# Opening of a conditioned transformer block: first norm's modulation first, weights of queries and keys split first, two constant rows set by ScalarE

## The chip, the cores and the metric

The kernel runs on one core of one Trainium2 chip. The metric is the device time of one execution in microseconds. The kernel is timed several times, and the median counts.

The engines, as the profile names them: PE is TensorE, DVE is VectorE, ACT is ScalarE, POOL is GpSimd, SP is SyncE, which only issues DMAs here. Each runs its own list of instructions in order, and they wait for each other by semaphores.

## The reference

One transformer block whose norms are modulated by a condition vector. There are 8 batches of 512 rows of 256 features, 16 heads of 16, and a hidden layer of 1024, all in float32:

```
c6 = silu(c) @ Wc + bc                              # c 8x256, Wc 256x1536
sh_msa, sc_msa, g_msa, sh_mlp, sc_mlp, g_mlp = split(c6, 6)
xm = layernorm(x) * (1 + sc_msa) + sh_msa
q, k, v = xm @ Wq + bq, xm @ Wk + bk, xm @ Wv + bv
w = softmax(q/16 @ k^T) per head;  y = w @ v
x = x + g_msa * (y @ Wo + bo)
xm2 = layernorm(x) * (1 + sc_mlp) + sh_mlp
x = x + g_mlp * (gelu(xm2 @ W1 + b1) @ W2 + b2)
```

The first two of the six vectors of `c6` (shift and scale of the first norm) are needed for the first batch's queries and keys. The other four are needed later.

## The kernel before, in words

**Steps.** `schedule` runs `step(i, par)` on every engine for i from -2 to 8. In step i the engines work on three batches at once: attention of batch i (transposed scores, exponentials, products with V), row maxima of the scores of batch i+1, norm and projections of batch i+2; the hidden layer of batch i-1 is in it too. The steps -2 and -1 are the fill: step -2 projects batch 0, step -1 projects batch 1 and then computes the scores and row maxima of half of batch 0's heads and a few more.

**Precision.** Operands of the projections are split in two: a rounded part (`hi`, type fp32r) and the rest (`lo`), and three products are summed. The split of the weights `wqkvo` is a cast and a subtraction on VectorE (lines 878 and 880). Queries and keys are each written as three bfloat16 parts: ScalarE takes the first from PSUM (L518), VectorE forms the remainder (L970) and the second part (L973), GpSimd the third (L438). SyncE stores them to DRAM (`parts_scratch`, `write_parts`, three DMAs for each of four tiles, L315) and loads them again in another order as the stacks `qst` and `kst` (`load_stack`, L322), 96 partitions deep. Two further rows of the stacks hold the row maxima, in `qst`, and the constant -1, in `kst`; only the transposed scores read them.

**Opening.** Before the steps, in the order of each engine:

- SyncE loads c, the two halves of Wc (rows 0 to 127 into `vaug[0]`, rows 128 to 255 into `qst[0]`, which are free until batch 0's V and queries), x of batch 0 (`xa`), bc, Wq, Wk, Wv, Wo, four small biases, W1, W2, and bo and b2 broadcast. Then it waits for `c6` and stores it (L274), for the gates that are read back later. In step -2 it loads x of batch 1 into the same `xa` when the transposes of batch 0 are done (L280), then come the stores of the parts.
- GpSimd sets the identity and small constants, then the two rows of -1 in `kst[0]` (L375), then the ones in `vaug[1]` (L377). When the modulation is done it sets the ones in `vaug[0]` (L407). It also raises variances to the power -1/2 (`norm`, L393).
- TensorE transposes c (L559), multiplies with Wc (L565: three chunks of 512 columns, two matmuls each, banks 1 to 3), transposes `c6` (L570, twelve small ones) and the biases (L574).
- VectorE finishes the silu (L814, L816, L818; ScalarE's exponential L458 lies ahead), does batch 0's statistics (L828) and variance (L834 to L839), adds bc (L868, 8x1536), normalises (L847), copies the modulation vectors (L872), adds 1 to both scales (L875), splits all four weights, and copies the biases (L883).
- ScalarE waits for the last of these (`prep_dve` 7) and writes z of batch 0, the modulated norm, from the transposed rows in PSUM (`modulate`, L478).

In step -2 VectorE goes on with the casts and the subtraction of z (`z_hi` L904, `z_lo` L908), then with statistics and variance of batch 1, then with the remainders of batch 0 (`rest_of`), then it normalises batch 1. TensorE does the projections of queries and keys (L700, L705) and V (L552). ScalarE writes V and then the rounded parts of W1 and W2 (L527, L528). The order is written out by hand; no planner sets it.

## Time and profile before

| | us |
|---|---|
| runs: median of 3 | 781.13 |
| runs: lowest, highest | 777.75, 783.33 |
| profiled execution, its own time | 775.7 |
| its span in the trace | 773.8 |
| TensorE busy | 707.6 (91%) |
| VectorE busy | 582.3 (75%) |
| ScalarE busy | 384.3 (50%) |
| GpSimd busy | 222.3 (29%) |

The profile is one execution, and times within it are microseconds from the start of its span. TensorE's busy time is an upper bound of its work, since matmuls are pipelined and their ends are modelled. The granted clock of TensorE has two levels, 1.2 and 2.4 GHz, shown as 0.50 and 1.00. A busy share is a mean over stages, so the opening has to be read from the chain of waits and the timeline.

### The profile page before, as it was taken

Reading aid. Unit: us, or ns where it says so; the run is one execution under the profiler, and the core shown is the slowest. Engines: PE = TensorE matmul, PEld = TensorE weight load, DVE = VectorE, ACT = ScalarE, POOL = GpSimd, SP = SyncE. Lnnn points to the kernel's source line nnn. Section 1 sums busy time; section 2 is a strip of 40 time slices with the busy share of each in tenths; the row PEclk is TensorE's granted clock in tenths of the full one; section 3 lists DMA queues with packets and bytes.
Section 4 is the critical chain, followed back from the end, with each engine's and each line's share of the span. In section 5 each row is a group of like instructions: output and inputs, shape, how many; then the busy total and the mean of one; then the engine's idle time right before and its main releaser. Section 6 shows DMA issues by size and latency. Waiting matters only on the chain.

```text
span 773.8 us, 11775 instructions
## 1 busy us (share of the span) xinstructions
PE 707.6 (91%) x3967; PEld 382.9 (49%) x3967; DVE 582.3 (75%) x1015; ACT 384.3 (50%) x462; POOL 222.3 (29%) x163
## 2 busy tenths in 40 slices
PE   4678989769999999999999899999999998998986
PEld 1551222432268425772378225862478225812976
DVE  5769688859886898789887798789886976721463
ACT  0430556217752676347642775257633773298221
POOL 5245001200334031511253032512162022230444
PEclk9785799959999999999999999999999999999998
DMA  8489100681039302860067303840076102021110
GB/s 290 138 253 289 62 21 22 223 203 55 28 136 261 99 28 73 257 165 34 31 218 176 112 15 121 247 141 28 30 243 166 59 27 72 3 82 45 56 35 27
DMA packets 59558, 88.45 MB, mean 114 GB/s; under 512 B 6214, under 2 KB 47708, under 8 KB 56428
## 3 DMA queue, kind: packets, MB, share of 16 engines
q1 hardware_dynamic: 59500, 87.69, 37.0%
q8 instruction: 35, 0.57, 0.3%
q14 instruction: 23, 0.19, 0.1%
HBM read 49.35 MB, written 38.06 MB: 113 GB/s over the span
## 4 chain that ended last, share of the span: by engine, by line
issue 34%; PE 32%; DVE 14%; POOL 11%; DMA 5%; ACT 3%; SPq 1%; POOLq 0%; DVEq 0%; ACTq 0%
DVE mx L899 7%; PE ps L620 7%; PE ps L598 7%; PE ps L628 6%; PE ps L552 5%; POOL hl L445 4%; PE ps L759 3%; POOL prob L438 2%; PE ps L763 2%; DMA qst<-mrow 2%; ACT prob L500 1%; DMA kst<-parts_scratch 1%; POOL x L418 1%; POOL xd L431 1%; POOL zl L397 1%
## 5 line engine op out<-in xcount | busy, mean ns | idle before, releaser
L899 DVE TENSOR_REDUCE mx<-ps 128x1 f32<-128x512 f32 x512 | 335.4, 685 | 62.6 <-PE ps L598 56.4
L500 ACT ACTIVATE prob<-ps 128x1024 f32<-128x1024 f32 x256 | 247.9, 1022 | 156.5 <-PE ps L628 156.2
L598 PE MATMUL ps<-kst,qst 96*128 96x512 bf16 x512 | 196.2, 405 | 24.9 <-DVE mx L899 19.0
L628 PE MATMUL ps<-qst,kst 98*128 98x512 bf16 x512 | 150.4, 385 | 4.0 <-DMA qst<-mrow 2.4
L598 PEld LDWEIGHTS ps<-kst,qst 96*128 96x128 bf16 x512 | 45.5, 98 | 191.5 <-DVE mx L899 165.8
L620 PE MATMUL ps<-prob,vaug 128*32 128x512 f32 x1024 | 137.6, 609 | 0.5 <-ACT prob L500 0.3
L445 POOL TENSOR_TENSOR hl<-z,hh 128x512 fp32r<-128x512 f32 x64 | 82.3, 1287 | 137.3 <-DVE hh L1028 137.3
L539 ACT ACTIVATE z<-ps,bias_t 128x512 f32<-128x512 f32 x64 | 44.1, 689 | 134.5 <-PE ps L763 127.1
L393 POOL TENSOR_TENSOR rstd<-vare,mhalf 128x4 f32<-128x4 f32 x16 | 16.4, 1022 | 249.6 <-DVE vare L839 249.6
L628 PEld LDWEIGHTS ps<-qst,kst 98*128 98x128 bf16 x512 | 46.9, 99 | 70.1 <-ACT prob L500 26.6
L438 POOL TENSOR_TENSOR prob<-prob 128x512 bf16<-128x512 f32 x32 | 37.4, 1167 | 139.7 <-DVE prob L973 139.7
L552 PE MATMUL ps<-w_hi,hh 128*128 128x256 f32 x256 | 73.6, 288 | 0.3 <-POOL hl L445 0.3
L552 PE MATMUL ps<-w_hi,hl 128*128 128x256 f32 x256 | 72.0, 281 | 0.0
L552 PE MATMUL ps<-w_lo,hh 128*128 128x256 f32 x256 | 71.9, 281 | 0.0
L1028 DVE CAST hh<-z 128x512 fp32r<-128x512 f32 x64 | 37.0, 580 | 35.8 <-ACT z L539 35.8
L759 PE MATMUL ps<-zh,w_hi 128*128 128x512 f32 x128 | 60.5, 472 | 2.0 <-DVE zh L904 2.0
L759 PE MATMUL ps<-zh,w_lo 128*128 128x512 f32 x128 | 51.5, 402 | 0.0
L552 PEld LDWEIGHTS ps<-w_hi,hh 128*128 128x128 f32 x256 | 48.2, 188 | 2.9 <-POOL hl L445 0.7
L552 PEld LDWEIGHTS ps<-w_lo,hh 128*128 128x128 f32 x256 | 48.2, 188 | 1.8
L552 PEld LDWEIGHTS ps<-w_hi,hl 128*128 128x128 f32 x256 | 48.2, 188 | 0.0
L620 PEld LDWEIGHTS ps<-prob,vaug 128*32 128x32 f32 x1024 | 20.4, 108 | 46.1 <-issue 41.9
L478 ACT ACTIVATE z<-ps,mod 128x512 f32<-128x512 f32 x30 | 21.7, 774 | 39.9 <-DVE bias_t L883 18.5
(106 smaller groups left out, 854.4 us busy)
## 6 DMA issues: line engine op xcount, KB each, us to landing
parts_scratch<-prob SPq DMA_DIRECT2D x32, 384.0 KB, 2.9
qst<-parts_scratch SPq DMA_DIRECT2D x16, 768.0 KB, 9.1
kst<-parts_scratch SPq DMA_DIRECT2D x16, 768.0 KB, 14.0
parts_scratch<-prob SPq DMA_DIRECT2D x32, 256.0 KB, 3.1
y_scratch<-rb SPq DMA_DIRECT2D x32, 256.0 KB, 2.0
xa<-in_x_dram SPq DMA_DIRECT2D x8, 512.0 KB, 4.4
parts_scratch<-prob SPq DMA_DIRECT2D x32, 128.0 KB, 2.9
xd<-in_x_dram SPq DMA_DIRECT2D x8, 512.0 KB, 3.5
```

The source lines that it names most:

```text
L438: pool.tensor_tensor(parts[:, j, PART_AT[j // 2][2], :], rest[:, j % 2, :], parts[:, j, 1, :], ALU.subtract).then_inc(part_l, 1)
L445: pool.tensor_tensor(hl[:, j % HR, :], hb[:, j % HB, :], hh[:, j % HR, :].bitcast(F32), ALU.subtract).then_inc(hl_done, 1)
L478: act.activation(z_of(n, b)[:, k, :], ps[:, banks + k, :], ACT.Identity, bias=mod[:, 2 * shift + k, bass.ds(b, 1)], scale=mod[:, 2 * scale ...
L500: act.activation(prob[:, s % 2, 2 * p:2 * p + 2, :], ps[:, 2 * p:2 * p + 2, :], ACT.Exp, scale=1.0 / DH).then_inc(exp_done, 1)
L539: act.activation(hb[:, j % HB, :], ps[:, 4 + j % 2, :], ACT.Gelu, bias=b1_t[:, j:j + 1]).then_inc(gelu_done, 1)
L552: m = pe.matmul(out_, a, b, start=start and n == 0, stop=stop and n == 2, skip_group_check=True)
L598: pe.matmul(ps[:, banks[n % len(banks)], :], qst[1 - par][0:MROW, h, t * P:(t + 1) * P], kst[1 - par][0:MROW, h, :], start=True, stop=True ...
L620: m = pe.matmul(ps[32 * q:32 * q + 32, 4 + g % 2, :], vaug[par][:, kt, G * g + q, :], prob[:, s % 2, q, :], start=kt == 0, stop=kt == TT - ...
L628: m = pe.matmul(ps[:, q, :], kst[par][0:KROWS, G * g + q, kt * P:(kt + 1) * P], qst[par][0:KROWS, G * g + q, :], start=True, stop=True)
L759: pe.matmul(ps[:, 4 + j % 2, :], w1[n][:, k, f], zh_of(1, b)[:, k, :], start=k == 0 and n == 0, stop=False)
L899: dve.tensor_reduce(mx[:, t, h:h + 1], ps[:, banks[n % len(banks)], :], AXX, ALU.max).then_inc(max_done, 1)
L1028: dve.tensor_copy(hh[:, j % HR, :], hb[:, j % HB, :]).then_inc(hh_done, 1)
```

## The change

- `kst[0]`'s two rows of -1 are no longer filled by GpSimd. ScalarE copies them from a constant column of -0.5 with scale 2, behind its exponential; a semaphore `krows_set` says so, and TensorE waits for it before the first transposed scores.
- The load of x goes ahead of Wc. Wc is loaded in two parts of columns: 0 to 511 (the first norm's shift and scale) early, 512 to 1535 behind Wq, Wk and the biases. Wv and Wo follow it.
- The modulation is computed in two turns. Chunk 0 comes first, with its sum (8x512), its four transposes and its vectors. Chunks 1 and 2 are multiplied in step -2 between the projections of keys and V (banks 6 and 7), their sum (8x1024) stands on VectorE behind the last remainder of batch 0, ahead of batch 1's normalising, and their eight transposes behind V.
- The split of the weights is in two halves: queries and keys before step -2's z, values and output behind batch 1's variance, ahead of batch 0's remainders.
- ScalarE's z waits for the first norm's vectors only, no longer for the splits and biases.
- SyncE's store of `c6` moves into step -2, behind the stores of batch 0's parts and ahead of the first stack loads; these also wait for the second turn of the modulation, since `qst[0]` holds Wc till then.
- GpSimd's fill of ones in `vaug[0]` moves behind its work on batch 0's parts.
- The silu's product is written into `yc` and not into z. General counters are replaced by semaphores for each purpose.

```diff
+MOD_BANKS = (1, 6, 7)
...
@@ SyncE
             sp.dma_start(stage[0:NB, 1, 0:H], c).then_inc(c_loaded, 16)
+            sp.dma_start(xa[:], x[0].rearrange("(t p) f -> p t f", p=P)).then_inc(xa_loaded, 16)
             for k in range(KC):
-                sp.dma_start(wc_half[k], Wc[k * P:(k + 1) * P, :]).then_inc(wc_loaded, 16)
-            sp.dma_start(xa[:], x[0].rearrange("(t p) f -> p t f", p=P)).then_inc(xa_loaded, 16)
+                sp.dma_start(wc_half[k][:, 0:2 * H], Wc[k * P:(k + 1) * P, 0:2 * H]).then_inc(wc_loaded[0], 16)
...
+            qkvo_weights(0, Wq, wqkvo_loaded[0])
+            qkvo_weights(1, Wk, wqkvo_loaded[0])
...
+            for k in range(KC):
+                sp.dma_start(wc_half[k][:, 2 * H:], Wc[k * P:(k + 1) * P, 2 * H:]).then_inc(wc_loaded[1], 16)
+            qkvo_weights(2, Wv, wqkvo_loaded[1])
+            qkvo_weights(3, Wo, wqkvo_loaded[1])
...
-            sp.wait_ge(prep_dve, 4)
-            sp.dma_start(c6_scr[:], stage[0:NB, 1, 256:256 + 6 * H]).then_inc(c6_written, 16)
+            def modulation_rows():
+                sp.wait_ge(c6_added, 2)
+                sp.dma_start(c6_scr[:], stage[0:NB, 1, 256:256 + 6 * H]).then_inc(c6_written, 16)
...
+                    if early(i) and not later(i, 2, 1):
+                        modulation_rows()
+                        sp.wait_ge(c6_done, 2)
                     load_stack(i + 2, 0, 0)
...
@@ GpSimd
-            pool.memset(kst[0][MROW:KROWS, :, :], -1.0).then_inc(const_set, 1)
+            pool.memset(vaug[1][:, :, :, DH:], 1.0).then_inc(const_set, 1)
...
                     norm(0, 0)
-                    pool.wait_ge(prep_pe, 2)
-                    pool.memset(vaug[0][:, :, :, DH:], 1.0).then_inc(const_set, 1)
                     norm(0, 1)
...
                         mlp_weights()
+                    elif early(i):
+                        pool.wait_ge(c6_done, 2)
+                        pool.memset(vaug[0][:, :, :, DH:], 1.0).then_inc(const_set, 1)
...
@@ ScalarE
+            act.wait_ge(const_set, 1)
+            act.activation(kst[0][MROW:KROWS, :, :], mhalf[MROW:KROWS, 0:1].unsqueeze(2).broadcast_to([KROWS - MROW, NH, S]), ACT.Copy,
+                           scale=2.0).then_inc(krows_set, 1)
...
                     if not later(i, 2, 1):
-                        act.wait_ge(prep_dve, 7)
+                        act.wait_ge(mod_set, 2)
                     modulate(0, i + 2, 2, SH1, SC1)
...
@@ TensorE
+            def modulation(chunks):
+
+                pe.wait_ge(wc_loaded[min(chunks[0], 1)], 16 * KC)
+                for n in chunks:
+                    for k in range(KC):
+                        m = pe.matmul(ps[0:NB, MOD_BANKS[n], :], yc[:, 1, k * NB:(k + 1) * NB],
+                                      wc_half[k][:, n * 512:(n + 1) * 512], start=k == 0, stop=k == KC - 1)
+                m.then_inc(c6_done, 1)
...
+            pe.wait_ge(silu_done, 3)
+            modulation((0,))
+            turn_modulation(1, 0, 4)
...
                     if not later(i, 2, 1):
                         pe.wait_ge(w_split, 2)
-                        pe.wait_ge(prep_dve, 7)
...
+                    if not later(i, 2, 1):
+                        modulation((1, 2))
+                        pe.wait_ge(w_split, 4)
                     for t in range(TT):
...
+                    if not later(i, 2, 1):
+                        turn_modulation(2, 4, 12)
...
@@ VectorE
+            def split_weights(turn):
+
+                w = slice(2 * turn, 2 * turn + 2)
+                src = stage[:, 0, 1024 * turn:1024 * turn + 1024]
+                dve.wait_ge(wqkvo_loaded[turn], 32)
+                dve.tensor_copy(wqkvo[0][:, w].rearrange("p n c f -> p (n c f)"), src).then_inc(w_split, 1)
...
             variance(0, 0)
...
+            add_c6(1, 0, (1,))
             for t in range(TT):
                 normalise(0, 0, xa, t)
...
+            set_modulation(1, 0, 4, SC1)
+            split_weights(0)
+            dve.wait_ge(bias_turned, 1)
...
                     for t in range(TT):
                         statistics(0, 1, xa, t)
                     variance(0, 1)
+                    split_weights(1)
...
                 if has_a and not later(i, 2, 1):
+                    add_c6(2, 512, (6, 7))
                     for t in range(TT):
                         normalise(0, 1, xa, t)
+                    set_modulation(2, 4, 12, SC2)
```

## Rows read from the trace of the kernel before

**Rows 1.** The page, its head: span and instructions.
```profile
span 773.8 us, 11775 instructions
```

**Rows 2.** Chain of waits, 0 to 110 us: start, us, what it is.
```profile
41.98 10.72 DMA kst<-parts_scratch
...
53.18 20.42 DVE mx L899 x34
```

**Rows 3.** Timeline, opening: start, us, engine, line, operation, count [idle before it <- releaser].
```profile
1.62 6.92 POOL L375 MEMSET kst<- 2x8192 bf16 x1
...
2.10 0.43 SPq L256 DMA_DIRECT2D xa<-in_x_dram  x1
...
4.41 4.16 DVE L814 TENSOR_SCALAR z<-z 128x16 f32<-128x16 f32 x1 [4.41 <-ACT z L458]
...
9.12 1.88 PE L565 MATMUL ps<-vaug,z 128*8 128x512 f32 x2 [6.31 <-DVE z L818]
...
11.67 0.43 SPq L271 DMA_DIRECT2D b_b<-in_L_cond_b_dram  x1
...
12.16 1.02 PE L565 MATMUL ps<-vaug,z 128*8 128x512 f32 x2
...
15.79 1.75 DVE L868 TENSOR_TENSOR qst<-ps,qst 8x1536 f32<-8x1536 f32 x1 [4.21 <-PE ps L565]
...
17.47 1.36 DVE L847 TENSOR_SCALAR xa<-xa,mv,rstd 128x256 f32<-128x256 f32 x4
...
18.89 1.97 PE L580 MATMUL ps<-ident,xa 128*128 128x128 f32 x8 [0.32 <-DVE xa L847]
...
19.19 1.22 DVE L878 CAST wqkvo_hi<-qst 128x2048 fp32r<-128x2048 f32 x1
20.45 2.29 DVE L880 TENSOR_TENSOR wqkvo_lo<-qst,wqkvo_hi 128x2048 fp32r<-128x2048 f32 x1
...
22.86 1.45 ACT L478 ACTIVATE z<-ps,mod 128x512 f32<-128x512 f32 x2 [18.48 <-DVE bias_t L883]
```

**Rows 4.** Timeline, 24 to 56 us: batch 0's projections to the first score.
```profile
25.94 1.40 DVE L828 BATCH_NORM_STATS2 stats<-xa 128x6 f32<-128x256 f32 x4
...
28.03 1.01 POOL L393 TENSOR_TENSOR rstd<-vare,mhalf 128x4 f32<-128x4 f32 x1 [11.26 <-DVE vare L839]
28.95 1.26 ACT L518 ACTIVATE prob<-ps,bias_t 128x512 bf16<-128x512 f32 x2 [4.65 <-PE ps L705]
...
29.67 0.75 DVE L970 SCALAR_TENSOR_TENSOR prob<-ps,bias_t,prob 128x512 f32<-128x512 f32 x1 [1.72 <-ACT prob L518]
...
32.16 7.20 SPq L315 DMA_DIRECT2D parts_scratch<-prob  x12
...
35.40 2.21 DVE L847 TENSOR_SCALAR xa<-xa,mv,rstd 128x256 f32<-128x256 f32 x4
...
35.62 1.90 ACT L527 ACTIVATE w_hi<-kst 128x2048 fp32r<-128x2048 f32 x1
...
52.75 1.56 PE L598 MATMUL ps<-kst,qst 96*128 96x512 bf16 x5 [1.10 <-DMA kst<-parts_scratch]
```

**Rows 5.** Timeline of ScalarE, 79 to 95 us: exponentials of batch 0.
```profile
83.50 1.94 ACT L500 ACTIVATE prob<-ps 128x1024 f32<-128x1024 f32 x2 [2.11 <-PE ps L628]
...
91.14 1.94 ACT L500 ACTIVATE prob<-ps 128x1024 f32<-128x1024 f32 x2 [1.15 <-PE ps L628]
```

**Rows 6.** Tile `xa`, 0 to 30 us: its two loads, issue to landing.
```profile
DMA to landing us min/median/max: 3.6/5.5/7.4
```

**Rows 7.** DMA issues by tile, 0 to 25 us: size, median us to landing.
```profile
b_b<-in_L_cond_b_dram SPq DMA_DIRECT2D x1, 128.0 KB, 6.3
```

**Rows 8.** Windows: stretch, busy PE, PEld, DVE, ACT, POOL, PEclk, DMA share, GB/s.
```profile
12.00:14.00 2.00, 2.00 (x6) 0.45 (x5) 0.00 (x0) 0.00 (x0) 0.77 (x1) 1.00 1.00 405
82.00:86.00 4.00, 4.00 (x16) 1.09 (x15) 2.51 (x4) 1.94 (x2) 0.00 (x0) 0.50 0.00 0
90.00:94.00 4.00, 3.91 (x24) 1.26 (x21) 3.00 (x5) 1.94 (x2) 0.00 (x0) 1.00 0.00 0
```

More of the change, by code:

```diff
@@ L135, in dit_block @@
         osb = xn[1]
-        c_loaded, wc_loaded, bc_loaded, bias_loaded = sem("c_loaded"), sem("wc_loaded"), sem("bc_loaded"), sem("bias_loaded")
-        wqkvo_loaded, wmlp_loaded, w_split = sem("wqkvo_loaded"), sem("wmlp_loaded"), sem("w_split")
+        c_loaded, bc_loaded, bias_loaded = sem("c_loaded"), sem("bc_loaded"), sem("bias_loaded")
+        wc_loaded = [sem("wc_loaded_first"), sem("wc_loaded_rest")]
+        wqkvo_loaded, wmlp_loaded = [sem(f"wqkvo_loaded_{n}") for n in ("qk", "vo")], sem("wmlp_loaded")
+        w_split, mlp_split = sem("w_split"), sem("mlp_split")
         c6_written, warm_set = sem("c6_written"), sem("warm_set")
-        const_set, ident_set, prep_dve, prep_pe, prep_act = (
-            sem("const_set"), sem("ident_set"), sem("prep_dve"), sem("prep_pe"), sem("prep_act"))
+        const_set, ident_set, krows_set = sem("const_set"), sem("ident_set"), sem("krows_set")
+        c_turned, c_exp, silu_done = sem("c_turned"), sem("c_exp"), sem("silu_done")
+        c6_done, c6_added, mod_turned, mod_set = sem("c6_done"), sem("c6_added"), sem("mod_turned"), sem("mod_set")
+        bias_turned, bias_set = sem("bias_turned"), sem("bias_set")
         xa_loaded = sem("xa_loaded")
@@ L349, in step @@
                     if early(i) and later(i, 2, 1):
[L350 removed]
+                        sp.wait_ge(const_set, 5)
                     load_stack(i + 2, 1, 0)
@@ L515, in step @@
                         act.wait_ge(qk_done, 4 * b + j + 1)
+                        if j == 0 and not later(i, 2, 1):
+                            act.wait_ge(bias_set, 1)
                         if later(i, 2, 1) and not runs(i, 0):
@@ L559, in _, with turn_modulation @@
                 m = pe.transpose(ps[:, 0, k * NB:(k + 1) * NB], stage[0:NB, 1, k * P:(k + 1) * P], ident[0:NB, 0:NB])
-            m.then_inc(prep_pe, 1)
-            pe.wait_ge(prep_dve, 3)
-            pe.wait_ge(wc_loaded, 16 * KC)
-            for n in range(3):
-                for k in range(KC):
-                    m = pe.matmul(ps[0:NB, 1 + n, :], z[0][:, 1, k * NB:(k + 1) * NB], wc_half[k][:, n * 512:(n + 1) * 512],
-                                  start=k == 0, stop=k == KC - 1)
-            m.then_inc(prep_pe, 1)
-            pe.wait_ge(prep_dve, 4)
-            for n in range(12):
-                m = pe.transpose(ps[:, 4, n * NB:(n + 1) * NB], stage[0:NB, 1, 256 + n * P:256 + (n + 1) * P], ident[0:NB, 0:NB])
-            m.then_inc(prep_pe, 1)
+            m.then_inc(c_turned, 1)
+            def modulation(chunks):
[5 more added lines that the diff above has]
+                m.then_inc(c6_done, 1)
+            def turn_modulation(turn, first, last):
+                pe.wait_ge(c6_added, turn)
+                for n in range(first, last):
+                    m = pe.transpose(ps[:, 0, 64 + n * NB:64 + (n + 1) * NB], stage[0:NB, 1, 256 + n * P:256 + (n + 1) * P], ident[0:NB, 0:NB])
+                m.then_inc(mod_turned, 1)
+            pe.wait_ge(silu_done, 3)
+            modulation((0,))
+            turn_modulation(1, 0, 4)
             pe.wait_ge(bias_loaded, 64)
             nb = 3 * KC + JT
-            pe.transpose(ps[:, 5, 0:nb], stage[0:nb, 1, 1792:1920], ident[0:nb, 0:nb]).then_inc(prep_pe, 1)
+            pe.transpose(ps[:, 1, 0:nb], stage[0:nb, 1, 1792:1920], ident[0:nb, 0:nb]).then_inc(bias_turned, 1)
             def transposes(n, b, bank):
@@ L648, in step @@
                     if not later(i, 0, 1):
-                        pe.wait_ge(const_set, 7)
+                        pe.wait_ge(const_set, 6)
+                        pe.wait_ge(krows_set, 1)
                         first_transposed(i, par)
@@ L810, in _ @@
         def _(dve):
[L812 removed]
+            dve.wait_ge(c_exp, 1)
             e = z[0][:, 0, 0:KC * NB]
[L814 to L818 removed]
+            dve.tensor_scalar(e, e, 1.0, None, ALU.add).then_inc(silu_done, 1)
+            dve.wait_ge(silu_done, 1)
+            dve.reciprocal(z[0][:, 0, 64:64 + KC * NB], e).then_inc(silu_done, 1)
+            dve.wait_ge(silu_done, 2)
+            dve.tensor_tensor(yc[:, 1, 0:KC * NB], ps[:, 0, 0:KC * NB], z[0][:, 0, 64:64 + KC * NB], ALU.mult).then_inc(silu_done, 1)
             def statistics(n, b, src, t):
@@ L859, in norm_piece, with add_c6, set_modulation @@
                     normalise(n, b, src, k - TT - 1)
+            def add_c6(turn, first, banks):
+                c6 = stage[0:NB, 1, 256 + first:256 + first + 512 * len(banks)]
+                dve.wait_ge(c6_done, turn)
+                dve.wait_ge(bc_loaded, 16)
+                dve.tensor_tensor(c6, ps[0:NB, banks[0]:banks[-1] + 1, :].rearrange("p n f -> p (n f)"), c6, ALU.add).then_inc(c6_added, 1)
+            def set_modulation(turn, first, last, scale):
+                dve.wait_ge(mod_turned, turn)
+                dve.tensor_copy(mod[:, first:last, :].rearrange("p n b -> p (n b)"), ps[:, 0, 64 + first * NB:64 + last * NB]).then_inc(mod_set, 1)
+                dve.wait_ge(mod_set, 2 * turn - 1)
+                dve.tensor_scalar(mod[:, 2 * scale:2 * scale + 2, :], mod[:, 2 * scale:2 * scale + 2, :], 1.0, None, ALU.add).then_inc(mod_set, 1)
+            def split_weights(turn):
[3 more added lines that the diff above has]
+                dve.tensor_copy(wqkvo[0][:, w].rearrange("p n c f -> p (n c f)"), src).then_inc(w_split, 1)
+                dve.wait_ge(w_split, 2 * turn + 1)
+                dve.tensor_tensor(wqkvo[1][:, w].rearrange("p n c f -> p (n c f)"), src,
+                                  wqkvo[0][:, w].rearrange("p n c f -> p (n c f)").bitcast(F32), ALU.subtract).then_inc(w_split, 1)
             for t in range(TT):
```

50 lines of the change are left out of this document (13 added, 37 removed).

## Prediction

> **What bounds the kernel now.** I read the page first, then the chain of waits, then the timeline of the opening, then the loads. The profiled execution took 775.7 us, of which the trace spans 773.8 [rows 1]; 1.9 us lie around it. Everything the change edits lies in the first 55 us: constants, modulation vectors, weight splits, and the projections of batches 0 and 1. The chain of waits runs through that stretch without a gap and comes out of it in one place: the load of the K stack that was issued at 41.98 and took 10.72 us, then the row maxima on VectorE, 34 of them in 20.42 us [rows 2]. So the opening is serial, and an earlier first score is worth its full amount: what follows (row maxima, batch loop, tail) is started by it and touched by no edit. The question is only how much earlier the stack loads can start.
>
> Follow the serial part backwards in the timeline [rows 3, 4]. The stack loads come behind twelve stores of parts, which SyncE issues from 32.16 for 7.20 us. The first store needs the first remainder on VectorE (29.67); that needs ScalarE's first part (28.95), that the first projection, and that batch 0's z, whose first instruction starts at 22.86. Two delays sit ahead of that z. One is 4.16 us for a 128x16 VectorE operation, starting at 4.41 and ending at 8.57: GpSimd's fill of two rows began at 1.62, lasted 6.92 us and ended at 8.54. The other is that z waits for the whole modulation (six matmuls, one 8x1536 sum) and then for the split of all four weights, 1.22 + 2.29 us on VectorE.
>
> **Part 1: the two rows go to ScalarE.** VectorE's operation falls from 4.16 to some 0.2 us; its two successors take 0.5 us more (9.12 is 0.55 behind 8.57), so the silu is ready at 5.1 instead of 9.1. The trace has no such ScalarE fill. ScalarE takes 1.94/2 = 0.97 us for 1024 elements [rows 5] and 1.90 for 2048 [rows 4], so 0.91 us per 1024; 8192 make 1.90 + 6 x 0.91 = 7.4 us, from 4.4 to 11.8. Bounds: 6.92 (GpSimd's own time) and twice mine, 15. I take 7.4 as the nearer; batch 0's z needs ScalarE at 13.5 (below), so it is hidden, and it starts to cost at 9.1 us.
>
> VectorE's operation ended 0.03 us behind the fill. The Trainium skill (SBUF — State Buffer, "SBUF: two separate sides") says why: VectorE and GpSimd share one port pair, held for a whole instruction. The trace agrees. The same rule speaks against a later piece of this change, in part 4.
>
> **Part 2: first chunk of the modulation.** The x load now goes ahead of Wc, and only Wc's first 512 columns are waited for: 8 + 512 + 512 KB. Before, x was third in line with 8 + 1536 KB ahead, issued at 2.10 and landed 7.4 later, at 9.5 [rows 3, 6]; in proportion, from a start of the stream at about 3, the first Wc part lands at 3 + 6.5 x 1032/2056 = 6.3. Two matmuls instead of six: the first pair of records began at 9.12 and the third at 12.16 [rows 3], so two matmuls are 3.0 us: 9.3. The sum over 512 instead of 1536 columns is 1.75/3 = 0.6: 10.0. Normalising is 1.36 (statistics and power are done by about 8.7): 11.4. Transposes take 1.97 as now, 13.4 to 13.5. Vectors of the first norm and half of the split, (1.22 + 2.29)/2 = 1.8 us, run on VectorE beside these and end near 13.9, before the z cast needs it. So z starts near 13.5, 9.4 us ahead of 22.86, and ScalarE's first part would let VectorE's first remainder start at 29.67 - 9.4 = 20.3.
>
> **Part 3: what is late next.** I do not expect the 9.4 to survive. VectorE works in order, and ahead of that remainder stand the statistics of batch 1, which read x of batch 1. That load goes out when batch 0's transposes end: before at 20.86, landing 3.6 later at 24.5 [rows 6], ahead of the statistics at 25.94. Now it goes out at 13.5, while the queue is still full of weights: b2 was issued at 11.67 and landed 6.3 later, at 18.0 [rows 3, 7]. The bytes of the opening are the same in the new order, so the queue drains at the same time, and x adds 0.52 MB at 405 GB/s [rows 8], 1.3 us: 19.1 to 19.3 at the end, I take 19.1. Bounds: 3.6 behind issue if nothing stood ahead (17.1), and 7.4, as for the first x (20.9).
>
> The Trainium skill (DMA: Bandwidth & Descriptors, "Queues, rings and completion order") says that descriptors on each DMA engine are consumed in ring order but completion isn't in order of issue. The first clause gives the 19.1, the second leaves room for the rival at 17.1.
>
> **Part 4: what VectorE now does before the remainder.** From the start of the statistics to the power on GpSimd are 28.03 - 25.94 = 2.1 us [rows 4]: 21.2. Then the second half of the split, moved in here, 1.8 us: 23.0. Before, there were 1.7 us of idle time at this spot, waiting for ScalarE; that cover is gone, since VectorE is now the late one. GpSimd's power (1.01) falls beside the split and can hold the subtraction for as long; between 0 and 1.0 I take 0.4. The first remainder starts at 23.5, 6.2 us ahead of 29.67.
>
> By the port rule of the skill page above, the power would block the subtraction, which reads two SBUF inputs, for its full 1.0 us; the sum would be 0.6 us worse.
>
> **Part 5: behind it.** Remainders, GpSimd's third parts and the stores keep their pace. Behind the twelfth store SyncE now also waits for the second half of the modulation and stores 48 KB: the wait is over by then (the four matmuls follow the K projection, and the sum stands on VectorE right behind the last remainder, while stores are still issued for several us). One issue more is 0.4 us, the queue is busy with stores beside it; from 0 to 0.4, I take 0.2. The stack loads start 6.0 earlier. Batch 1's projections must end before the first score. TensorE stood idle for 1.10 us there [rows 4]; that is their slack. Ahead of their normalising now stands a sum of 2/3 x 1.75 = 1.2 us, and GpSimd's fill of ones, moved here, may hold VectorE up to 1 us more. ScalarE's MLP weights (two of 1.90 from 35.62) ended at 39.4 and covered 0.4 us. So batch 1 is 0.8 to 1.8 late against a slack of 1.1: cost 0 to 0.7, I take 0.3. The four extra matmuls sit before V, which isn't late: TensorE has run ahead of VectorE by 3 us. Waits on split semaphores and other banks cost nothing: their producers are long done.
>
> **Sum.** 6.2 - 0.2 - 0.3 = 5.7 us less. On the profiled execution 775.7 - 5.7 = 770.0; on the median of the runs shown, 5.4 us above that execution, 781.1 - 5.7 = 775.4. With the low and the high ends of the parts (x at 17.1 or 20.9; 0 or 1.0; 0 or 0.4; 0 or 0.7) the gain is 8.6 or 2.7.
>
> **Rivals.**
> *The x load isn't held by the queue.* It lands at 17.1; the remainder starts 2.0 earlier, gain 7.7: 773.4. For it: completion out of order; against: x waited 7.4 us in the full queue the first time. If also the split costs nothing, 8.6: 772.5.
> *The fill on ScalarE is slow.* At 15 us it ends at 19.4, and z starts there instead of at 13.5: 3.5 us ahead of before, less 0.5: gain 3.0, 778.1. For it: two partitions only, a 16-bit output and a repeated source, none of which a row shows; against: GpSimd's 6.92.
> *The change doesn't do what it says: the 4.16 us aren't the fill's.* Then the silu is at 9.1, two matmuls end at 12.1, z starts at 16.3, VectorE reaches the statistics at 19.4, behind x by 0.3. The gain would be 5.4: 775.7. It can't be told by the time, only by the row of that operation.
> *Slower: the low clock reaches further into batch 0's attention.* A step of it takes 1.94 + 2.11 = 4.05 us between 82 and 86, where the granted clock is 0.50 (1.2 GHz), and 1.94 + 1.15 = 3.09 where it is 1.00, 2.4 GHz [rows 5, 8]: 0.96 a step. Before the fall TensorE had been paced by row maxima. If it came back later, six more of the 16 steps would eat the gain, and ten would give 781.1 - 5.7 + 9.6 = 785.0. For it: the maxima stage stays as thin as it is; against: it is moved whole, so the low stretch should move with it.
>
> **How the numbers follow.** Forecast 0.66; x early 0.16; slow fill 0.08; change not as said 0.04; slower by the clock 0.06. The runs of before spread over 5.6 us, so a measurement tells about 1%, 7.8 us, from no change. Forecast, slow fill and the fourth case lie within 1%, apart from some 0.11 that noise carries over on the fast side; x early lies on the line and goes mostly to faster. That gives faster 0.25, same 0.71, slower 0.04. The range runs from 770.5 (x early with noise) to 779.0 (slow fill with noise).
>
> **What would show it.** The first small VectorE operation at 0.2 us instead of 4.16; batch 0's z at 13 to 14; a wait of VectorE of 2 to 3 us for x of batch 1 at about 16.5 to 19; the first remainder at 23 to 24; the first score near 46.7 instead of 52.75. Wrong if x lands before 18, if ScalarE's fill is over 9 us, or if the first score is outside 44 to 50. If the first score is early as said and the time is not, the loss is behind it, and the granted clock is where I would look.

## The result, and the profile after

The kernel before took 779.88 us and the changed kernel 776.03 us, each the median of 14 runs. The ratio is 0.9937 with a 95% interval of 0.9922 to 0.9951: faster by 0.6%, or 4.9 us by the ratio (3.8 to 6.1) and 3.85 us by the medians. Forecast were 5.7 us less and 775.4. The profile of each kernel is of one of its quickest executions: 772.2 us is the lowest of the 14 of the changed kernel, and the 775.7 us of the kernel before lie below all 14 of that one.

The head of the page of the changed kernel; [rows 1] had 773.8:

```profile
span 770.0 us, 11786 instructions
```

The timeline of its opening (start, us, engine, line, operation, count, and in brackets the idle time before it with what ended it). It answers [rows 3].

```profile
4.27 7.02 ACT L477 ACTIVATE kst<-mhalf 2x8192 bf16<-2x8192 f32 x1
4.28 0.17 DVE L850 TENSOR_SCALAR z<-z 128x16 f32<-128x16 f32 x1 [4.28 <-ACT z L475]
...
7.30 1.87 PE L589 MATMUL ps<-vaug,yc 128*8 128x512 f32 x2 [4.62 <-DMA qst<-in_L_cond_Wc_dram]
...
10.91 0.68 DVE L903 TENSOR_TENSOR qst<-ps,qst 8x512 f32<-8x512 f32 x1 [4.03 <-PE ps L589]
...
12.68 0.43 SPq L284 DMA_DIRECT2D b_b<-in_L_cond_b_dram  x1
...
12.93 1.97 PE L611 MATMUL ps<-ident,xa 128*128 128x128 f32 x8 [0.58 <-DVE xa L883]
...
13.81 1.22 DVE L919 TENSOR_TENSOR wqkvo_lo<-qst,wqkvo_hi 128x1024 fp32r<-128x1024 f32 x1
14.93 0.38 SPq L294 DMA_DIRECT2D xa<-in_x_dram  x1
...
15.00 1.45 ACT L498 ACTIVATE z<-ps,mod 128x512 f32<-128x512 f32 x2 [3.71 <-PE ps L611]
```

VectorE's first small operation takes 0.17 us where it took 4.16. ScalarE's fill of the two rows takes 7.02 us and ends at 11.3, ahead of z at 15.00. The first modulation matmul starts at 7.30, and what it waited for is no longer VectorE but the load of Wc. z of batch 0 starts at 15.00 instead of 22.86. The load of batch 1's x goes out at 14.93.

The timeline further on, batch 0's remainders and batch 1's norm, which answers [rows 4]:

```profile
20.36 1.26 ACT L540 ACTIVATE prob<-ps,bias_t 128x512 bf16<-128x512 f32 x2 [3.91 <-PE ps L736]
...
22.08 1.41 DVE L864 BATCH_NORM_STATS2 stats<-xa 128x6 f32<-128x256 f32 x4 [3.91 <-DMA xa<-in_x_dram]
...
24.18 1.39 POOL L409 TENSOR_TENSOR rstd<-vare,mhalf 128x4 f32<-128x4 f32 x1 [16.12 <-DVE vare L875]
...
24.73 1.22 DVE L919 TENSOR_TENSOR wqkvo_lo<-qst,wqkvo_hi 128x1024 fp32r<-128x1024 f32 x1
...
25.88 0.74 DVE L1019 SCALAR_TENSOR_TENSOR prob<-ps,bias_t,prob 128x512 f32<-128x512 f32 x1
...
28.36 7.37 SPq L329 DMA_DIRECT2D parts_scratch<-prob  x12
...
30.69 1.90 ACT L549 ACTIVATE w_hi<-kst 128x2048 fp32r<-128x2048 f32 x1
...
31.59 1.21 DVE L903 TENSOR_TENSOR qst<-ps,qst 8x1024 f32<-8x1024 f32 x1
31.75 2.21 POOL L452 TENSOR_TENSOR prob<-prob 128x512 bf16<-128x512 f32 x1 [0.36 <-DVE prob L1022]
...
32.73 3.23 DVE L883 TENSOR_SCALAR xa<-xa,mv,rstd 128x256 f32<-128x256 f32 x4
...
33.91 0.94 POOL L457 MEMSET vaug<- 128x1024 f32 x1
```

ScalarE's first part starts at 20.36, and VectorE could have begun its remainder at 21. It begins at 25.88. The bracket of the statistics tells why: VectorE sat idle for 3.91 us until x of batch 1 had landed, and behind the landing stood statistics, variance and the second half of the split. The first store goes out at 28.36, 3.80 us earlier than before (32.16).

The last piece, to the first score:

```profile
35.77 0.55 SPq L288 DMA_DIRECT2D c_scratch<-qst  x1
...
36.10 1.94 PE L611 MATMUL ps<-ident,xa 128*128 128x128 f32 x8 [2.30 <-DVE xa L883]
...
36.43 0.79 SPq L336 DMA_DIRECT2D qst<-parts_scratch  x2
37.26 2.16 SPq L336 DMA_DIRECT2D kst<-parts_scratch  x2
38.08 1.44 ACT L498 ACTIVATE z<-ps,mod 128x512 f32<-128x512 f32 x2 [3.69 <-PE ps L611]
...
49.66 1.04 PE L629 MATMUL ps<-kst,qst 96*128 96x512 bf16 x4
```

Tile `kst` in the window from 36 to 41 us, its two loads, issue to landing:

```profile
DMA to landing us min/median/max: 12.2/12.5/12.7
```

The first score is at 49.66, 3.09 us ahead of 52.75. Its bracket is empty: TensorE went over from batch 1's V without waiting, where it had waited 1.10 us for a stack. It needs the first K stack, and that one, issued at 37.26, had landed 12.2 us later, at 49.44, 0.2 ahead of the score; before it landed at 52.70 (41.98 + 10.72, [rows 2]). So the 3.8 us at the first store are 3.3 at the landing of the stack and 3.1 at the first score. The first loss, 0.5, is in stores and loads of the parts. The twelve stores took 7.37 us instead of 7.20, and the store of `c6` stands behind them (35.77), so that the stack loads begin at 36.43, 3.0 us earlier and not 3.8. The second, 0.2, is batch 1's projections, which end just behind the stack. They had lost most of their lead on VectorE: the sum of the second half (1.21) now stands ahead of batch 1's normalising, and that took 3.23 us (2.21 before), beside GpSimd's last part (2.21) and the fill of ones (0.94). The transposes behind it ran at the low clock, 1.94 us.

Three windows (busy PE, PEld, DVE, ACT, POOL; then granted clock, DMA share, GB/s):

```profile
16.00:18.00 2.00, 1.55 (x4) 1.29 (x5) 1.79 (x3) 0.45 (x1) 0.00 (x0) 1.00 1.03 360
18.00:20.00 2.00, 2.00 (x8) 1.58 (x7) 0.17 (x1) 0.00 (x0) 0.00 (x0) 1.00 0.66 174
34.00:36.00 2.00, 0.00 (x0) 0.00 (x0) 2.00 (x5) 0.39 (x1) 0.85 (x1) 0.50 1.09 383
```

The queue of the opening still moves 174 GB/s from 18 to 20 us, where the kernel before moved 25. At 34 to 36 us the granted clock is 0.50, the lower level (1.2 GHz), and TensorE is idle, as it has been since 30.2 us but for eight small transposes (0.94 us from 32.85).

How the gain passes on is read from GpSimd's powers, one at the end of the opening and one a step later. First the kernel before, then the changed one:

```profile
114.42 1.01 POOL L393 TENSOR_TENSOR rstd<-vare,mhalf 128x4 f32<-128x4 f32 x1 [45.43 <-DVE vare L839]
...
183.64 1.02 POOL L393 TENSOR_TENSOR rstd<-vare,mhalf 128x4 f32<-128x4 f32 x1 [35.11 <-DVE vare L839]
```

```profile
111.34 1.01 POOL L409 TENSOR_TENSOR rstd<-vare,mhalf 128x4 f32<-128x4 f32 x1 [43.92 <-DVE vare L875]
...
179.61 1.02 POOL L409 TENSOR_TENSOR rstd<-vare,mhalf 128x4 f32<-128x4 f32 x1 [34.16 <-DVE vare L875]
```

From the first score to the first of these are 61.67 us before and 61.68 after: the 3.1 us arrive in full. At the second the lead is 4.03. The further 0.94 fall between 145 and 180 us, in a stretch at the low clock whose length differs between profiles (below): from 170 to 175 us the granted clock was 0.72 before and 1.00 after.

### The profile page after: what moved, and what is told of

Its sections match the earlier page's. It is cut to its first block, busy times and chain, and to the rows that moved or that the text cites. A ratio compares the mean times of both kernels' runs of the same rounds, so it can differ in the third digit from the quotient of the medians.

```text
span 770.0 us, 11786 instructions
## 1 busy us (share of the span) xinstructions
PE 709.4 (92%) x3967; PEld 382.9 (50%) x3967; DVE 580.5 (75%) x1019; ACT 391.1 (51%) x463; POOL 216.5 (28%) x162
## 4 chain that ended last, share of the span: by engine, by line
PE 35%; issue 34%; DVE 14%; POOL 11%; ACT 3%; DMA 3%; POOLq 0%; SPq 0%; ACTq 0%; DVEq 0%
DVE mx L947 7%; PE ps L651 7%; PE ps L629 7%; PE ps L574 6%; PE ps L659 5%; POOL hl L462 4%; PE ps L795 4%; PE ps L799 2%; POOL prob L452 2%; ACT prob L520 2%; DVE prob L1019 1%; POOL x L432 1%; POOL xd L445 1%; PE ps L611 1%; PE ps L731 1%
## 5 line engine op out<-in xcount | busy, mean ns | idle before, releaser
L629 PE MATMUL ps<-kst,qst 96*128 96x512 bf16 x512 | 197.5, 407 | 22.5 <-DVE mx L947 17.1
L799 PE MATMUL ps<-zl,w_hi 128*128 128x512 f32 x128 | 41.5, 407 | 0.1
```

The lines of the kernel that those rows point to most:

```text
L629: pe.matmul(ps[:, banks[n % len(banks)], :], qst[1 - par][0:MROW, h, t * P:(t + 1) * P], kst[1 - par][0:MROW, h, :], start=True, stop=True ...
L799: m = pe.matmul(ps[:, 4 + j % 2, :], w1[0][:, k, f], zl_of(1, b)[:, k, :], start=False, stop=k == KC - 1)
```

## The experiments

Theory A, formed on the trace above: the pace of the opening is set by a chain that goes from the landing of batch 1's x over VectorE to the stores; what the change gained ahead of this chain is hidden by it. Theory B: the gain comes from the fill on ScalarE. Theory C: beyond a point batch 1's projections, not batch 0's, set the first score. D and E concern the rate of the queue.

### The fill back on GpSimd

```diff
-            act.activation(kst[0][MROW:KROWS, :, :], mhalf[MROW:KROWS, 0:1].unsqueeze(2).broadcast_to([KROWS - MROW, NH, S]), ACT.Copy,
-                           scale=2.0).then_inc(krows_set, 1)
+            pool.memset(kst[0][MROW:KROWS, :, :], -1.0).then_inc(krows_set, 1)
+            pool.wait_ge(krows_set, 1)
```

> The changed kernel with the two rows of -1 filled by GpSimd again, as before; nothing else. Theory A (the load of batch 1's x sets the pace): VectorE's first small operation again takes about 4.2 us, the first modulation matmul starts at 9.1 instead of 7.3 and z of batch 0 at 16.8 instead of 15.0, but batch 1's x lands where it did, near 22, behind the weights in the queue, so the first remainder stays at 25.9 and the time is that of the changed kernel within 0.5 us (about 0.994 of before). Theory B (the fill on ScalarE is where the gain comes from): all of the 1.8 us arrives at the first remainder (27.7) and in the time (about 0.996 to 0.997).

Measured: 775.24 us, ratio 0.994 (0.9922 to 0.9958), the same as the changed kernel. Its timeline:

```profile
4.42 4.14 DVE L849 TENSOR_SCALAR z<-z 128x16 f32<-128x16 f32 x1 [4.42 <-ACT z L477]
...
9.12 1.88 PE L588 MATMUL ps<-vaug,yc 128*8 128x512 f32 x2 [6.29 <-DVE yc L853]
...
16.83 1.45 ACT L497 ACTIVATE z<-ps,mod 128x512 f32<-128x512 f32 x2 [12.44 <-PE ps L610]
...
22.62 1.41 DVE L863 BATCH_NORM_STATS2 stats<-xa 128x6 f32<-128x256 f32 x4 [2.63 <-DMA xa<-in_x_dram]
...
26.43 0.74 DVE L1018 SCALAR_TENSOR_TENSOR prob<-ps,bias_t,prob 128x512 f32<-128x512 f32 x1
```

The 4.14 us are back when GpSimd fills, so it is that fill which holds VectorE. The Trainium skill (SBUF — State Buffer, "SBUF: two separate sides") tells of a port pair that VectorE and GpSimd share and that one holds for a whole instruction; the traces agree, 0.17 us without the fill and 4.14 with it. z is 1.83 us later than in the changed kernel, and the first remainder only 0.55 (26.43 against 25.88), because VectorE waits 2.63 us for x instead of 3.91. A stands, B falls: the change's most visible repair is worth nothing measurable in its own surroundings. The first K stack landed at 49.38, as in the changed kernel (49.44). The first score of this profile came later all the same (51.10 against 49.66): batch 1's first matmuls were longer at the low clock (0.50 up to 45 us, there up to 43). The profiled execution, 777.7 us, is 2.5 above the median of its kernel, and the median shows no such loss.

### The fill alone, in the kernel before

```diff
-            pool.memset(kst[0][MROW:KROWS, :, :], -1.0).then_inc(const_set, 1)
+            act.wait_ge(const_set, 1)
+            act.activation(kst[0][MROW:KROWS, :, :], mhalf[MROW:KROWS, 0:1].unsqueeze(2).broadcast_to([KROWS - MROW, NH, S]), ACT.Copy,
+                           scale=2.0).then_inc(krows_set, 1)
```

> The kernel before with only the fill of the two rows moved to ScalarE. Before, nothing waits for x of batch 1, so what the silu gains reaches the first remainder, up to the landing of Wc. Theory A: the silu is ready at 5.1, the modulation starts when Wc has landed, at 7.6 instead of 9.1, and the first remainder is at 28.2 instead of 29.7: time 1.5 us less (0.998). Theory B: all 4 us of the operation are gained (0.995). A third outcome, no gain at all (1.000), would say that something else holds z.

Measured: 779.23 us, ratio 0.999 (0.997 to 1.001). Its timeline:

```profile
7.89 1.87 PE L566 MATMUL ps<-vaug,z 128*8 128x512 f32 x2 [5.16 <-DMA qst<-in_L_cond_Wc_dram]
...
28.63 0.75 DVE L972 SCALAR_TENSOR_TENSOR prob<-ps,bias_t,prob 128x512 f32<-128x512 f32 x1 [1.71 <-ACT prob L519]
```

The modulation starts 1.2 us earlier, when Wc has landed, and the first remainder 1.04 (28.63 against 29.67). At the first score only 0.14 were left (52.61 against 52.75): from the first store to the landing of the first K stack it took 21.4 us here and 20.5 before. Why the loads took longer is open. A's size for the remainder was 1.5; the interval of the time holds both 1 us and nothing. Four us (B, 0.995) it was not.

### The second half of the split ahead of the wait

```diff
+                    split_weights(1)
                     for t in range(TT):
                         statistics(0, 1, xa, t)
                     variance(0, 1)
-                    split_weights(1)
```

> The changed kernel with the second half of the weights' split on VectorE ahead of batch 1's statistics, where VectorE sits idle for 3.9 us waiting for x, instead of behind the variance. Theory A (what stands on VectorE behind the landing of x is on the path): the first remainder moves from 25.9 to 24.0, the first score from 49.7 to 47.8, the time 1.9 us less (0.991 to 0.992 of before). Theory C (batch 1's projections are bound by something else, TensorE or ScalarE, not by VectorE's chain): the first remainder moves, the first score doesn't, time as the changed kernel.

Measured: 774.11 us, ratio 0.9927 (0.9905 to 0.9948). Its timeline:

```profile
21.95 1.40 DVE L864 BATCH_NORM_STATS2 stats<-xa 128x6 f32<-128x256 f32 x4 [2.79 <-DMA xa<-in_x_dram]
...
23.89 0.74 DVE L1019 SCALAR_TENSOR_TENSOR prob<-ps,bias_t,prob 128x512 f32<-128x512 f32 x1
...
47.49 1.04 PE L629 MATMUL ps<-kst,qst 96*128 96x512 bf16 x4
```

The remainder is at 23.89, 1.99 us earlier, and the first score at 47.49 instead of 49.66, 2.17 earlier. That is A's forecast (24.0 and 47.8) to a few tenths, by moving one call into idle time. The medians differ by 1.9 us; the intervals of the two ratios overlap, so the time alone would not settle it, and the trace does.

### Batch 1's x loaded early

```diff
+            sp.dma_start(x1[:], x[1].rearrange("(t p) f -> p t f", p=P)).then_inc(xb_loaded, 16)
...
-                if runs(i, 2) and later(i, 2, 1) and not early(i) or early(i) and not later(i, 2, 1):
+                if runs(i, 2) and later(i, 2, 1) and not early(i):
...
-                        statistics(0, 1, xa, t)
+                        statistics(0, 1, x1, t)
...
-                        normalise(0, 1, xa, t)
+                        normalise(0, 1, x1, t)
```

> The changed kernel with x of batch 1 loaded into a free tile (x1) in the opening, behind the biases and ahead of the rest of Wc, so that its statistics don't wait for the load. Theory A: VectorE goes from the z split at 18.2 straight to the statistics, the first remainder is at 22.2 instead of 25.9, the first score at 46 instead of 49.7, the time 3.6 us less than the changed kernel (0.989 of before). Theory C (something else holds batch 1's projections or the stacks): first remainder near 22, first score later than 48, and under 1.5 us gained.

Measured: 774.17 us, ratio 0.9925 (0.9906 to 0.9944). Its timeline:

```profile
22.01 0.75 DVE L1024 SCALAR_TENSOR_TENSOR prob<-ps,bias_t,prob 128x512 f32<-128x512 f32 x1
...
32.23 1.09 PE L613 MATMUL ps<-ident,xa 128*128 128x128 f32 x8
...
34.04 1.90 ACT L552 ACTIVATE w_hi<-kst 128x2048 fp32r<-128x2048 f32 x1
35.84 1.44 ACT L500 ACTIVATE z<-ps,mod 128x512 f32<-128x512 f32 x2
...
48.36 1.57 PE L631 MATMUL ps<-kst,qst 96*128 96x512 bf16 x5
```

(The new load stands behind those of the biases, ahead of the rest of Wc, and x lands at 10.3.) The remainder is where A put it, at 22.01. The first score is not: 48.36 instead of 46, so C holds from here on. The first K stack landed at 45.30, 3.1 us ahead of the score, so it is batch 1's projections that are late. The gain in time, 0.9 us by the ratios and 1.9 by the medians, fits C's 1.5 better than A's 3.6. The rows name the place. TensorE's transposes of batch 1 are done at 33.3, and ScalarE's z starts at 35.84, right behind the rounded MLP weights, which it takes first and which end there. In the kernel before the same two instructions held z by 0.4 us at most (TensorE's transposes ended at 38.82, z started at 39.22).

### The same, with the MLP weights behind batch 1's z

```diff
-                if early(i) and not later(i, 2, 1):
+                if early(i) and later(i, 2, 1):
                     act.wait_ge(wmlp_loaded, 64)
                     act.activation(w1[0][:].rearrange("p c f -> p (c f)"), mlp_stage[:, 0:2048], ACT.Copy).then_inc(mlp_split, 1)
                     act.activation(w2[0][:].rearrange("p c f -> p (c f)"), mlp_stage[:, 2048:4096], ACT.Copy).then_inc(mlp_split, 1)
```

The block stands right behind `modulate(0, i + 2, ...)`, on top of the edits of the run before.

> The kernel with x of batch 1 loaded early (the run before this one gained 1.3 us at the first score where 3.6 were expected; batch 1's z stood on ScalarE, ready at its input at 33.3, behind V and the two rounded MLP weights, 32.2 to 35.8), and besides with these two moved behind batch 1's z, where ScalarE waits 4.5 us for the projections. If ScalarE's order was what held it: z of batch 1 at 33.4 instead of 35.8, first score 46.0 instead of 48.4, time 2.4 us less than with the early x alone (0.989 to 0.990 of before). If TensorE's clock or the stacks hold it, the first score stays above 47.5.

Measured: 770.99 us, ratio 0.9891 (0.9855 to 0.9927). ScalarE's row:

```profile
33.23 1.45 ACT L500 ACTIVATE z<-ps,mod 128x512 f32<-128x512 f32 x2 [2.18 <-PE ps L612]
```

z is 2.6 us earlier, the first score at 45.68, 2.7 earlier, and the time 3.2 us less than with the early x alone (2.7 by the ratios, whose intervals overlap). ScalarE's order was what held it. A repeat, in the last pair of runs, gave 770.34 and 0.9876 (0.9834 to 0.9919). Both ratios lie below the 0.9925 of the early x alone.

### GpSimd's ones later

```diff
-                    elif early(i):
-                        pool.wait_ge(c6_done, 2)
-                        pool.memset(vaug[0][:, :, :, DH:], 1.0).then_inc(const_set, 1)
```

In the changed kernel; the two lines go to the head of `mlp_weights`, in step -1.

> The changed kernel with GpSimd's fill of ones in vaug[0] moved from behind batch 0's last part to step -1, ahead of the MLP weights. In the changed kernel batch 1's normalising on VectorE took 3.23 us, beside GpSimd's last part (2.21 us) and the fill (0.94). Theory A (the fill holds VectorE, on the path of batch 1's projections, which set the first score): normalising 2.2 us instead of 3.2, first score 48.7 instead of 49.7, time 1.0 us less than the changed kernel. Rival (other work covers it: ScalarE's MLP weights end at 34.4, TensorE's transposes wait for all of it anyway): nothing.

Measured: 776.00 us, ratio 0.9951 (0.9932 to 0.9971), no gain. Normalising took 2.35 us instead of 3.23, so the fill did hold VectorE for 0.9. The statistics of batch 1, which wait for its x, began at 22.58 instead of 22.08, and z of batch 1 still 0.4 us earlier (37.69 against 38.08). Behind it the gain was lost: the granted clock stayed at 0.50 up to 44 us instead of 43, and the first score was at 50.01. As a saving in time it is not shown; it is below what a run tells.

### Wc loaded whole

```diff
-                sp.dma_start(wc_half[k][:, 0:2 * H], Wc[k * P:(k + 1) * P, 0:2 * H]).then_inc(wc_loaded[0], 16)
+                sp.dma_start(wc_half[k], Wc[k * P:(k + 1) * P, :]).then_inc(wc_loaded[0], 16)
...
-                sp.dma_start(wc_half[k][:, 2 * H:], Wc[k * P:(k + 1) * P, 2 * H:]).then_inc(wc_loaded[1], 16)
```

> The changed kernel with Wc loaded whole (rows of 6 KB) behind x, instead of in two parts of columns (2 KB and 4 KB). It asks why the queue drained later than forecast (b2 landed at 20.6 instead of 18.0). Theory D (the cut rows make the loads slower): b2 lands near 18 and x of batch 1 near 19.5. Theory E (the rate of the queue is another matter, the cut costs nothing): b2 lands at 20 to 21, x of batch 1 near 22. In both, the first modulation matmul starts later, at 9.1 to 9.5 instead of 7.3, and z at 17. Time by D 1 to 2 us less than the changed kernel; by E the same or up to 1 us more.

Measured: 775.32 us, ratio 0.9947 (0.9922 to 0.9971). Windows and timeline:

```profile
16.00:18.00 2.00, 1.85 (x8) 1.45 (x8) 1.97 (x4) 0.05 (x1) 0.00 (x0) 1.00 0.75 245
18.00:20.00 2.00, 0.60 (x2) 0.54 (x3) 1.03 (x4) 1.39 (x2) 0.00 (x0) 1.00 0.45 122
```

```profile
10.24 1.87 PE L587 MATMUL ps<-vaug,yc 128*8 128x512 f32 x2 [7.54 <-DMA qst<-in_L_cond_Wc_dram]
...
17.88 0.38 SPq L292 DMA_DIRECT2D xa<-in_x_dram  x1
...
21.50 1.41 DVE L862 BATCH_NORM_STATS2 stats<-xa 128x6 f32<-128x256 f32 x4 [0.39 <-DMA xa<-in_x_dram]
```

The queue moves 245 and 122 GB/s in the windows where the changed kernel moved 360 and 174, so it had less left; b2 was issued at 11.78 and landed 7.0 later, at 18.8, against 12.68 and 7.9, 20.6. By the drain of the queue D holds, for 1.8 us. But half of that is there at b2's issue already, and the run takes away two loads and moves the later columns of Wc ahead, besides leaving the rows whole; which of the three counts it doesn't separate. And x of batch 1 can't use the gain: it is issued at 17.88, when the transposes are done, and lands 3.5 later, at 21.4 and not near 19.5 as D said. The first matmul is later than either theory had it, at 10.24. Early Wc columns cost the queue 1.8 us and give the first matmul 2.9 (7.30 against 10.24); both kernels arrive at the statistics at nearly the same time, 22.08 and 21.50, and at the same time of execution, where D had forecast 1 to 2 us less. The part of the change that loads the columns early gains nothing as long as x of batch 1 stands where it does.

### All late things together

Early x; Wv and Wo rounded by ScalarE and their rest by GpSimd; MLP weights, ones and the store of `c6` late; and, for batch 0:

```diff
-            add_c6(1, 0, (1,))
             for t in range(TT):
                 normalise(0, 0, xa, t)
+            add_c6(1, 0, (1,))
...
             modulation((0,))
+            transposes(0, 0, 2)
             turn_modulation(1, 0, 4)
```

> All that the trace of the changed kernel shows as late, together: x of batch 1 loaded early, the split of Wv and Wo on ScalarE (rounded) and GpSimd (rest), the MLP weights behind batch 1's z, GpSimd's ones and SyncE's store of c6 later, and batch 0's normalising and transposes ahead of the sum and the turn of the first modulation chunk. Theory A (the chain norm, projections, parts, stacks sets the first score, all else is cover): z of batch 0 at 13.3, first remainder at 19.5 to 20, first score at 43 to 44, 6 us ahead of the changed kernel, time 0.986 to 0.987 of before. Rival (the clock): a gain at the first score is partly given back in the next 130 us, in stretches at the low clock, and the time is 0.989 to 0.991.

Measured: 772.13 us, ratio 0.990 (0.9869 to 0.9931). z started at 13.41, the first remainder at 20.80, the first score at 45.26, where TensorE had waited 2.13 us for a stack: from the first store (23.28) to the landing of the first K stack it took 21.9 us, against 21.1 in the changed kernel. So the projections of batch 1 are no longer last; stores and loads of the parts are. A's first score, 43 to 44, was missed by over 1 us. The time is in the rival's range, but its reason isn't shown, since the first score itself was late. It isn't faster than the two edits above.

### Four edits, and the two again

Early x, late MLP weights, late ones, and batch 0's transposes ahead of the sum; the split and the store of `c6` as in the changed kernel.

> The early x and the late MLP weights, and besides GpSimd's ones late and batch 0's normalising and transposes ahead of the first chunk's sum and turn; the split of Wv and Wo stays on VectorE and the store of c6 ahead of the stack loads. With the two edits alone the first store was at 24.4 and the first score at 45.7, TensorE's projections of batch 1 setting it. From the first store to the end of the stack loads it has been 23 us in nearly all traces. Theory A: first store at 23.3, first score at 43.8 to 44.5, time 1 to 1.5 us less than with the two edits. Rival (as with all edits together, the stack loads then take longer, or the clock gives it back): first score above 45 and no difference in time.

> The kernel with the early x and the late MLP weights once more, on the same chip as the kernel with four edits, to be compared with it. The same as in its first run: first score near 45.7, 0.989 of before.

Measured: 770.18 us, ratio 0.9874 (0.9833 to 0.9915), and 770.34 us, ratio 0.9876 (0.9834 to 0.9919). First scores, of the four edits and of the two:

```profile
43.47 1.56 PE L631 MATMUL ps<-kst,qst 96*128 96x512 bf16 x5 [1.35 <-DMA kst<-parts_scratch]
```

```profile
44.57 1.56 PE L630 MATMUL ps<-kst,qst 96*128 96x512 bf16 x5 [1.25 <-DMA kst<-parts_scratch]
```

Both now wait for a stack. The four edits put the first store at 22.93 and the first score at 43.47, a little ahead of the forecast; the two have 24.46 and 44.57. The 1.1 us between them are not seen in the times, so A's 1 to 1.5 us less did not come. They are no more than what the kernel with the two edits shows between its own two profiles (45.68 and 44.57). The clock speaks for the rival: the mean granted clock of the six runs was 0.9485 with four edits and 0.9543 with two, and in the profiles the step behind the opening (next section) took 71.1 against 68.6 us. One pair of profiles does not show it to be the edits' doing. The version to keep is the simpler one, with two edits: early x and late MLP weights, 9 us less than the kernel before.

### What moves between profiles

The stretch at the low clock that begins between 141 and 152 us, in batch 0's step, did not end at the same point in all profiles. The window 166 to 174 of the changed kernel, and of the kernel with the fill back on GpSimd (columns as above):

```profile
166.00:174.00 8.00, 6.01 (x35) 2.61 (x39) 3.95 (x5) 4.94 (x6) 0.00 (x0) 0.99 0.28 57
```

```profile
166.00:174.00 8.00, 5.93 (x23) 4.16 (x22) 0.56 (x1) 1.94 (x2) 0.00 (x0) 0.50 0.42 91
```

With clock 0.99 and 0.50 there, the step between the two GpSimd powers took 68.3 us in the first and 70.9 in the second (112.97 to 183.83). The kernel before had 69.2, and all twelve profiles lie between 68.3 and 71.2. None of the edits touches this stretch. The longer stretch goes with the longer step, so a single profile may differ by 1 to 3 us on its account, as much as one of the smaller edits is worth, and that is why first store and first score are compared here beside the times.

Taken together the runs bear out that an earlier first score is worth its full amount. The first scores of the twelve profiles lie between 43.5 and 52.8 us, and the median time of the runs less the first score of the profile between 724 and 727.

## Why the prediction was right, and where its terms were off

The direction, the size within its range and the place were right: the time is 0.6 us above the forecast, by the medians. That it came so near is luck. The gain by the medians was 3.85 us and not 5.7, and the forecast was counted from 781.13, the median of the three runs shown, while 14 runs of the same kernel gave 779.88; the 1.25 us between the two hide most of the shortfall. The terms, in the order of the prediction:

- **Part 1, the two rows.** The silu's operation fell to 0.17 us as said, and ScalarE's fill took 7.02 where 7.4 were taken, hidden as said. That the fill of GpSimd was the cause is shown by putting it back. That it would hardly matter for the time followed from the rival in which the 4.16 us aren't the fill's (gain 5.4 instead of 5.7), and the run with the fill back bears it out (0.994 against 0.9937).
- **Part 2, the first chunk.** z at 15.0, not 13.5. Wc's columns landed at 7.2 instead of 6.3, and two matmuls took 3.6 us instead of 3.0 (7.30 to 10.9). The price for two matmuls had been read from rows where the second of them already ran faster. This error of 1.5 us was covered by part 3: with the fill back z came 1.8 us later still, and x landed only 0.5 later.
- **Part 3, what is late next.** It was the main step, and its mechanism held: VectorE waited 3.91 us for batch 1's x (2 to 3 were forecast), and the first remainder came 3.8 us earlier, where 6.2 were forecast. The term was mis-sized. x landed at 22.0, 2.9 us behind the 19.1 taken and outside the bounds of 17.1 to 20.9. The step that failed is "The bytes of the opening are the same in the new order, so the queue drains at the same time": b2 landed at 20.6, not 18.0, and with Wc whole at 18.8. The 1.3 us for x behind it were right (1.37). That x was issued at 14.93 instead of 13.5 did not count. In the runs with the ones late, the split early and the fill back, whose loads are the same, it was issued at 13.91, 14.06 and 16.76 us, and landed at 22.49, 21.86 and 22.53, each time 1.35 to 1.36 us behind b2. The rival in which x isn't held by the queue is out.
- **Part 4, VectorE's chain.** Statistics to remainder took 3.8 us, and 4.3 were taken (19.1 + 4.3 make 23.4; the 23.5 there is 0.1 too late). GpSimd's power did not hold the subtraction (1.22 us, as in the first half); it was itself drawn out from 1.01 to 1.39. The Trainium skill (SBUF — State Buffer, "SBUF: two separate sides") gives the port pair to whichever operation starts first, and here VectorE's cast had begun first (24.02, the power 24.18), which fits the power's delay. But the subtraction began at 24.73, beside a power that ran to 25.57, and was not held: the full block that the prediction took from the page is not in the trace. The doubt of 1.0 us was not needed. The run with the split ahead of the wait shows the 1.9 us of that split on the path.
- **Part 5, behind it.** From the first store to the first K stack 0.5 us were lost (3.80 ahead at the first store, 3.26 at that landing), where 0.2 were taken; the store of `c6` and its issue lie in it, and no run moves that store alone. The last of the four stack loads landed 3.74 ahead, so the loads as a whole took no longer. Batch 1's projections cost 0.2 where 0.3 were taken. By its own sum the prediction's first score should have stood at 47.05 (52.75 - 5.7); its "near 46.7" leaves out the 0.3 for the projections.

In sum the first score came 3.1 us earlier where 5.7 were forecast; nearly all of the 2.6 between them is x's landing. The profiled span is 3.8 us shorter, since the low-clock stretch behind the opening was shorter in that profile. The interval of the ratio, 3.8 to 6.1 us, lies above the 3.1 of the opening. That part of the gain is not explained by an edit. The 3.1 are read from one profile of each kernel, and two profiles of one and the same kernel differed by 1.1 us in the first score, so much of the gap may be that. The clock's stretches behind the opening are the other candidate. The mean granted clock of the 14 runs was 0.949, against 0.945 and 0.946 in two sets of 23 runs of the kernel before, but in the profiles that difference lies ahead of the first score (0.90 against 0.84) and so in the 3.1 already. Neither is shown over many profiles.

## What to carry to other kernels

When a change speeds up a serial opening, find the first thing on the next engine that does not move with it, here a load that can only be issued when its buffer is free and then stands behind the weights; its landing, and not the work removed, sets the gain. Work that fills idle time (a weight split, a cast on ScalarE) must be looked at again after each such change, since it becomes the path as soon as its cover goes: in these runs moving one call gave 2 us, moving two casts 3. Put a load that the next batch needs ahead of weights that are needed later, into another tile if its own isn't free.

## What was not expected of the hardware

- The same bytes in the queue took longer when Wc was cut into rows of 2 and 4 KB: b2 landed at 20.5 to 21.2 us in the four kernels with that list of loads, and at 18.0, 18.8 and 18.9 in the three with whole rows of 6 KB. Between 4 and 8 us the queue moved 309 to 347 GB/s in the changed kernel, against 366 to 396 with Wc whole; there Wq and Wk also come up earlier, so the landing is the cleaner number. That the rows are the cause is argued: the cut also adds two loads and moves a part of Wc behind others.
- How late a load was issued into the full queue made no difference: x of batch 1, issued between 13.9 and 16.8 us, landed 1.35 to 1.37 us behind b2 in four kernels.
- From the first store of batch 0's parts to the landing of the first K stack it took 20.1 to 21.1 us in ten of twelve profiles, and once the projections are out of the way this is the floor of the opening. The other two had 21.4 (the fill alone) and 21.9 (all edits together), with no cause found.
- An edit can be plain in the trace and nothing in the time: 4 us of VectorE for 0, 0.9 us of normalising for 0.
